# Cross attention and a 4-bit feed-forward layer on one core: block turns of the row and weight tiles by VectorE, their high parts stored by ScalarE

## The reference

```python
x = x + xattn(layernorm(x), ctx, ctx, mask, wq, wk, wv, wo)   # 32 query heads, 8 key heads of 128, rotary embedding, softmax
x = x + ffn(layernorm(x), qweight, lut4, lut8, bias)          # weights looked up from bit planes: 4 bits per weight
```

## Time and profile before

| | us |
|---|---|
| median of the runs before (3 runs) | 2351.77 |
| lowest and highest run | 2350.05, 2352.4 |
| span of the profiled execution | 2348.6 |
| median above that span | 3.17 |
| TensorE busy | 2330.7 (99%) |
| VectorE busy | 1690.5 (72%) |
| ScalarE busy | 1115.5 (47%) |
| GpSimd busy | 570.1 (24%) |

### The profile page before, as it was taken

One profiled execution on the slowest core, in us unless ns is written; L12 is line 12 of the kernel. 1 busy time (PEld: TensorE's weight loads), 2 busy tenths in 40 slices (PEclk: granted clock), 3 DMA queues, 4 the chain that ended last, 5 costly groups with the idle time before them and its releaser, 6 DMA issues.

```text
span 2348.6 us, 35132 instructions
## 1 busy us (share of the span) xinstructions
PE 2330.7 (99%) x11878; PEld 1989.3 (85%) x11878; DVE 1690.5 (72%) x3808; ACT 1115.5 (47%) x2469; POOL 570.1 (24%) x674
## 2 busy tenths in 40 slices
PE   9999999999999999999999999999999999999999
PEld 8999998788888888888888888888888888888787
DVE  7888777677776767777776767676777777776773
ACT  5555544555464646455544445444544444443110
POOL 1000001222232223232322232223323232322220
PEclk9999999999999999999999999999999999999999
DMA  7466558533344343434457633333333333335442
GB/s 258 159 199 213 190 177 299 170 109 117 115 133 120 109 127 111 129 107 128 117 162 238 209 104 115 90 112 109 112 93 113 105 100 111 107 93 185 122 142 81
DMA packets 330098, 328.26 MB, mean 140 GB/s; under 512 B 32448, under 2 KB 266176, under 8 KB 329920
## 3 DMA queue, kind: packets, MB, share of 16 engines
q1 hardware_dynamic: 294496, 309.88, 42.8%
q10 hardware_dynamic: 35424, 16.14, 2.6%
HBM read 181.73 MB, written 71.30 MB: 108 GB/s over the span
## 4 chain that ended last, share of the span: by engine, by line
PE 92%; DVE 3%; DMA 3%; ACT 1%; SPq 1%; issue 1%; POOL 0%; ACTq 0%; DVEq 0%
PE bank L829 28%; PE bank L915 28%; PE bank L845 7%; PE bank L886 7%; PE bank L783 7%; PE bank L955 7%; PE bank L760 7%; DMA small_split<-probs 1%; DMA k_scratch<-small_split 1%; SPq L615 0%; POOL probs L1930 0%; DMA small_split<-k_scratch 0%; DVE residual L1804 0%; PE bank L721 0%; PE bank L741 0%
## 5 line engine op out<-in xcount | busy, mean ns | idle before, releaser
L915 PE MATMUL bank<-weights_split,small_split 128*128 128x512 f32 x3072 | 741.0, 390 | 1.9 <-DVE small_split L1788 1.9
L829 PE MATMUL bank<-acts_split,weights_split 128*128 128x512 f32 (+1 forms) x3168 | 742.9, 384 | 0.0
L915 PEld LDWEIGHTS bank<-weights_split,small_split 128*128 128x128 f32 x3072 | 574.4, 188 | 121.6 <-DVE small_split L1788 3.2
L829 PEld LDWEIGHTS bank<-acts_split,weights_split 128*128 128x128 f32 x3168 | 575.1, 188 | 110.6
L1930 POOL TENSOR_SCALAR probs<-probs,row_numbers 128x256 f32<-128x256 f32 x512 | 359.3, 714 | 1192.9 <-DVE row_numbers L1774 1192.9
L1248 ACT ACTIVATE probs<-bank,row_numbers 128x256 f32<-128x256 f32 x512 | 238.1, 472 | 125.2 <-DVE row_numbers L1769 125.0
L1778 DVE STREAM_TRANSPOSE probs<-probs 128x512 f32<-128x512 f32 x250 | 177.7, 711 | 145.2 <-POOL probs L1930 145.2
L1922 POOL TENSOR_TENSOR rope_x<-rope_x,sin_t 128x512 f32<-128x512 f32 (+1 forms) x132 | 166.7, 1263 | 404.7 <-ACT rope_x L1221 404.5
L1763 DVE CUSTOM_DVE_ANT_0 bank<-bank,mask_tile 128x256 f32<-128x256 f32 x512 | 207.2, 447 | 64.5 <-PE bank L845 64.4
L1783 DVE TENSOR_TENSOR small_split<-small_split 128x512 fp32r<-128x512 f32 x250 | 178.8, 715 | 85.2 <-ACT small_split L1261 85.0
L845 PEld LDWEIGHTS bank<-small_split 128*128 128x128 f32 x1536 | 217.6, 190 | 23.0 <-DVE small_split L1743 1.6
(11 more groups left out here) (124 smaller groups left out, 2167.0 us busy)
## 6 DMA issues: line engine op xcount, KB each, us to landing
small_split<-probs SPq DMA_DIRECT2D x754, 64.0 KB, 2.2
raw<-in_L_xattn_wq SPq DMA_DIRECT2D x61, 512.0 KB, 3.8
raw<-in_L_xattn_wo SPq DMA_DIRECT2D x60, 512.0 KB, 3.8
k_scratch<-small_split SPq DMA_DIRECT2D x64, 256.0 KB, 2.3
v_scratch<-small_split SPq DMA_DIRECT2D x32, 512.0 KB, 2.9
x_scratch<-raw SPq DMA_DIRECT2D x64, 256.0 KB, 2.8
acts_split<-x_scratch SPq DMA_DIRECT2D x32, 512.0 KB, 5.0
mask_tile<-in_mask_BxSxS_ff SPq DMA_DIRECT2D x64, 256.0 KB, 3.0
```

What stands on the lines that cost most here:

```text
L829: last = pe.matmul(query_bank(j)[:, 0:wide], wq_s[:, h, c, a, :], xT[:, c, m, b * S:b * S + wide], start=c == 0 and i == 0, stop=c == C - ...
L915: last = pe.matmul(out_ps[part][:, :], o_s[:, a, u % 2 * S + t * P:u % 2 * S + (t + 1) * P], wo_s[:, h, m, n * BANK:(n + 1) * BANK], start ...
```

## The change

Rows 0 to 7 and all eight weight tiles are no longer turned by TensorE. VectorE turns each in two instructions, straight from the tile into two PSUM banks, in blocks of 32 x 32, reading the columns in an order (`block_order`) by which the blocks need no transpose of their own; each 32-row part is then stored by one DMA that spreads 32 partitions over 128 lines of 1 KB. The copies in DRAM and in `W` and `X` are laid out accordingly, the query products of the first half and the final layer's products read them in runs of 32 columns. The high part is stored first, by four DMAs that ScalarE issues after both of its copies, the low part by four DMAs of SP; both parts use one staging area in turn. Row 8 and the rows of the attention stage stay as they were. In the final layer, the first row's products are ordered by half, and the second row is turned after 32 of them.

```diff
 # ScalarE
+            def send_blocks(image, at, src, done):
+                for a in range(PARTS):
+                    act.dma_start(image[:, at + a * S:at + (a + 1) * S], src[a * QUAD:(a + 1) * QUAD, :]).then_inc(done, 16)
+            def blocks_high(e):
+                act.wait_ge(x_tr, 2 * e + 2)
+                act.wait_ge(x_stored, rows_stored(e))
+                for j in range(2):
+                    act.activation(x_split[:, j, :], x_ps[j][:, :], ACT.Copy).then_inc(x_hi, 1)
+                act.wait_ge(x_hi, 2 * e + 2)
+                send_blocks(x_blocks, (e // REP * 2 + HI) * REP * D + e % REP * D, raw, x_stored)
+                def weights_high(tile):
+                    act.wait_ge(w4_tr, 2 * tile + 2)
...
+                    for j in range(2):
+                        act.activation(weight_stage(tile, HI)[:, j * BANK:(j + 1) * BANK], w4_ps[j][:, :],
+                                       ACT.Copy).then_inc(w4_hi, 1)
+                    act.wait_ge(w4_hi, 2 * tile + 2)
+                    send_blocks(w_scr, (tile // REP * 2 + HI) * REP * D + tile % REP * D,
+                                weight_stage(tile, HI).bitcast(F32), w4_stored)
...
                 if b - 1 in V_ROW:
-                    x_high(V_ROW[b - 1], 0, x_ps[0])
+                    blocks_high(V_ROW[b - 1])
                 rope_swap(b * HKV, k_ps[0], 1.0, 0, 2)
...
                     if not (first or last) and g == TURN_AT[b]:
-                        weights_high(b - 1, D0)
-                    if not (first or last) and g == SECOND_AT[b]:
-                        weights_high(b - 1, D1)
+                        weights_high(b - 1)
                     if g + 1 < HKV:
                         rope_swap(b * HKV + g + 1, k_ps[(g + 1) % 2], 1.0, (g + 1) % 2, 2)
...
                         act.wait_ge(v_stored, 16 * (v_turn(b, i) + 1))
+                        act.wait_ge(w4_stored, 16 * 2 * PARTS * b)
...
 # VectorE
+            def turn_weight_blocks(tile):
+                dve.wait_ge(w4_ready, tile + 1)
+                dve.wait_ge(w4_lo, 2 * tile)
+                for j in range(2):
+                    dve.transpose(w4_ps[j][:, :], block_order(picks[0], j)).then_inc(w4_tr, 1)
+            def weights_low(tile):
+                dve.wait_ge(w4_hi, 2 * tile + 2)
+                if tile < NB - 1:
+                    dve.wait_ge(w4_stored, 16 * PARTS * (2 * tile + 1))
...
+                    if g == TURN_AT[b] - 1:
+                        turn_weight_blocks(b - 1)
                     if g == SECOND_AT[b]:
-                        weights_low(b - 1, D1)
+                        weights_low(b - 1)
...
+                if b in K_ROW and K_ROW[b] < HT:
+                    turn_row_blocks_early(K_ROW[b])
                 values_low(V0)
...
+                if b in V_ROW:
+                    turn_row_blocks_early(V_ROW[b])
                 values_low(V3)
 # TensorE
-                    if not (first or last) and g == TURN_AT[b]:
-                        turn_weights(b - 1)
...
-                if b in V_ROW:
-                    turn_row(V_ROW[b])
...
-                        xT[:, c, m, b * S:b * S + wide],
+                            moving = xT_blocks[:, b // 2, m, c, b % 2 * C:b % 2 * C + wide // QUAD]
...
+                if f == 0:
+                    products = [(0, c, k) for c in range(C) for k in range(3)]
+                    products += [(1, c, k) for c in range(C) for k in (0, 2)] + [(1, c, 1) for c in range(C)]
...
+                    if f == 0 and (n, c, k) == (1, C // 2 - 1, 2) and PE_ROWS > 1:
+                        turn_rows(1)
```

More of the change, by code:

```diff
@@ L734, in turn_rows @@
                 last.then_inc(ln_tr, 1)
-            def turn_weights(tile):
-                pe.wait_ge(w4_ready, tile + 1)
-                pe.wait_ge(stage_lo, STAGED // 2 + tile * STAGED)
-                for c in range(C):
-                    done = pe.transpose(w4_ps[c // 4][:, (c % 4) * P:(c % 4 + 1) * P],
-                                        picks[0][:, c * P:(c + 1) * P], ident[:, :])
-                    if c % 4 == 3:
-                        done.then_inc(w4_tr, 1)
             def batch(b, first=False, last=False):
@@ L794, in batch @@
                 values(0)
-                if b in K_ROW:
+                if b in K_ROW and K_ROW[b] >= HT:
                     turn_row(K_ROW[b])
@@ L948, in _ @@
                     pe.wait_ge(wide_free, B_WIDE - A_WIDE + f * NN + n + 1)
-                columns = [(n, c) for n in range(NN) for c in range(C)] if f == NT - 1 else [
-                    (n, c) for c in range(C) for n in range(NN)]
-                for n, c in columns:
-                    if f == 0 and n == 0:
-                        pe.wait_ge(w4_in[c], 16)
-                    for i, (a, m) in enumerate(PASSES):
-                        last = pe.matmul(out_ps[f % 2 * NN + n][:, :],
-                                         xT[:, c, a, f % HT * P:(f % HT + 1) * P],
-                                         w4_s[:, c, m, n * BANK:(n + 1) * BANK],
-                                         start=c == 0 and i == 0, stop=c == C - 1 and i == 2)
-                    if c == C - 1:
+                if f == 0:
+                    products = [(0, c, k) for c in range(C) for k in range(3)]
+                    products += [(1, c, k) for c in range(C) for k in (0, 2)] + [(1, c, 1) for c in range(C)]
+                elif f == NT - 1:
+                    products = [(n, c, k) for n in range(NN) for c in range(C) for k in range(3)]
+                else:
+                    products = [(n, c, k) for c in range(C) for n in range(NN) for k in range(3)]
@@ new lines, in _ @@
+                ends = [max(at for at, product in enumerate(products) if product[0] == n) for n in range(NN)]
+                for at, (n, c, k) in enumerate(products):
+                    a, m = PASSES[k]
+                    if f == 0 and at == 0:
+                        for piece in range(C // 2):
+                            pe.wait_ge(w4_in[piece], 16)
+                    if f == 0 and n == 1 and c == 0 and k < 2:
+                        for piece in range(2):
+                            pe.wait_ge(w4_in[C // 2 + 2 * k + piece], 16)
+                    last = pe.matmul(out_ps[f % 2 * NN + n][:, :],
+                                     xT[:, c, a, f % HT * P:(f % HT + 1) * P], w4_s[:, n, m, c],
+                                     start=c == 0 and k == 0, stop=at == ends[n])
+                    if at == ends[n]:
@@ L1707, in batch @@
                 values_low(V1)
-                if b in K_ROW:
+                if b in K_ROW and K_ROW[b] < HT:
+                    blocks_low(K_ROW[b])
+                elif b in K_ROW:
                     x_low(K_ROW[b], 1, x_ps[1])
```

205 lines of the change are left out of this document (107 added, 98 removed).

## The result

The changed kernel takes 2421.26 us (median of 4 runs, 2420.54 to 2425.06), the kernel before 2351.23 beside it: a ratio of 1.0297, with a 95% interval of 1.0282 to 1.0311. It is slower, by 70 us where 20 were forecast, and outside the range.

The account below looks back on a forecast made before the run. TensorE, busy 99% of the span, was taken to bound the kernel. New waits of 34.1 us less 13.9 us of turns removed gave +20 us on a median of 2351.8: 2372 us, range 2354 to 2384.

Parts of the forecast that it names:

- the mechanism of the waits: Projection stage: VectorE's turns and ScalarE's copies and 2.5 us issue burst delay the swap and cosine product that TensorE's key groups need.
- the first rival: ScalarE's bursts: issuing does not hold ScalarE, so waits of groups 2 to 4 vanish; 2345 us, chance 0.14.
- the second: ScalarE's bursts: an issue takes only 0.36 us, a burst 1.45; 2363 us, chance 0.15.
- batch 1: Projection stage: value product V2 starts late, behind VectorE's low parts and a landing store; 5.4 us.
- batch 2: Projection stage: row centring, bit copy and burst in one group delay key group 6, and V0's low part is late; 4.8 us.
- batch 6: Projection stage, one weight tile: the burst makes key group 4 stall 2.1 us.
- final layer: Second row turned after 32 products instead of 24: 1.8 us more, the third row's wait 4 us instead of 2.3.
- Batch 3: Projection stage: waits at key groups as in batch 4 (6.3 us), with the context copy 1 us later; 7.0 us.
- The contiguous loads I cost at nothing: Contiguous loads and wider store lines: no cost, since no wait for such a load stands in the chain.
- the sign of a wrong forecast: Attention stage: no difference expected; time coming there would show the forecast wrong.
- The third rival: VectorE becomes the bound at 1.9 us a pair, +9, 2381 us; or runs of 32 slow 1,536 query products, 6 us; chance 0.13.
- the pair of turns: VectorE: two block turns of 512 columns take 1.25 us, 20 us in all, with 1.9 us as the far end.

Follow-up runs that it names:

- e11: Kernel before, with 1,152 query products reading runs of 64 columns and 720 final products runs of 128: 2352.7 us.
- e7: Changed kernel with VectorE's turns reading 512 columns in one run instead of every fourth column: 2412.2 us.
- e1: Changed kernel with the four issues of each high part moved from ScalarE to SP's queue: 2394.9 us.
- e3: Changed kernel with the turns given back to TensorE, ScalarE's bursts of issues kept: 2395.5 us.
- e5: Changed kernel with both the high parts issued by SP and the turns given back to TensorE: 2380.6 us.
- e12: Changed kernel with SP's issues, turns and reads in one run, second final-layer row turned after 24 products, and row turns ahead of decoding: 2359.6 us.
- e9: Changed kernel with extra unread matmuls filling 16 of TensorE's waits in the projection stage: 2417.2 us.
- e6: Kernel before, with 1,152 query products and 720 final products reading 16 runs of 32 columns instead of one of 512: 2368.3 us.
- e8: Changed kernel with twelve test turns on VectorE at the start and the second final-layer row turned after 24 products: 2424.8 us, one run.
- e4: Changed kernel with each high part stored by one DMA of ScalarE over 128 partitions instead of four over 32: 2455.0 us.
- after: The changed kernel itself, as profiled, against the kernel before: 2421.3 us.

## Why the prediction was wrong, step by step

**Right.** The sign, and the mechanism of the waits: ScalarE is held (swap 0.1 us behind the last issue), which rules out the first rival; an issue takes 0.63 us, which rules out the second; the bursts took 2.5 to 2.8 us (four of the 16 3.0 to 4.1), and in four places the waits came as worked out: batch 1 6.3 us (5.4 forecast), batch 2 6.9 (4.8), batch 6 2.5 (2.1), final layer 3.7 (about 4). In all 40.4 us of new waits in the projection stage against 32.3. Batch 3, 6.9 against 7.0, is luck: 2.9 of it stand in front of key group 0, where none was forecast, and 4.0 at the groups that were to have it all. Of what the Trainium skill says (DMA: Bandwidth & Descriptors, Issuing engines are not separate DMA queues), that the time of an issue is "usually small relative to the DMA itself", the trace shows 0.63 beside 3.3 us to landing, and 14.8 us of the whole for 64 issues on the engine that others wait for: the rows were the better guide.

**Wrong, first: a term that was left at nothing.** "The contiguous loads I cost at nothing" looked at the loads, and the reads of TensorE in runs of 32 had a place only in a rival, at 4 ns over 1,536 products. The runs show 10 ns over 2,304: about 23 us, nearly half of the 49 us that were missed, most of it in the attention stage, where time was to be the sign of a wrong forecast. The 4 ns came from L886, which reads runs of 64; e11 shows that query products in runs of 64 cost nothing more, so that row said little of runs of 32. The third rival named both this and the dearer pair of turns, as alternatives to the forecast; both came on top of it.

**Wrong, second: the pair of turns.** 1.25 us was taken and 1.9 called the far end; it was 2.1 to 2.2. Both nearest rows read their columns in one run; the strided read was named in the prediction and given no price. e7: 9.0 us.

**Wrong, third: the sum of waits taken place by place.** The forecast counted the stall of each group from an engine that starts each batch on time. But VectorE had little room (busy 39.5 of 44.7 us in batch 1), and the burst and the turns together cost 11.5 us more than each alone (e1, e3, e5). The late turn of a row, with the next load, V1's copy and the next row's statistics behind it, was never followed, and the wait for the landing of the high part was named for the weight tiles and not for the rows. Both stand in the chain behind the 7.7 us of waits at the heads of batches 3 to 5; moving the turn forward gave back 4.3 (e12).

**Wrong, fourth: the clock, which had no term.** Behind most waits of 2 to 6 us the granted clock was at its lower level for a while (not behind the 2.54 us of batch 6), and key and value products took 14.7 us more. Of these 4 are shown to be time of the whole (e9), as a lower bound; for most of the rest the other engines were as late anyway.

The projection stage's 44 us are about 26 more than forecast. Read from the trace, 8.1 of them are waits, 14.7 longer key and value products, and some 3 are not placed. By the runs, the turns' price (9.0), the earlier turn (4.3) and the clock (4.1) make 17, if they may be added; that the rest is lateness which the two loads pass on to each other is argued from e1, e3 and e5 and not taken apart further.

## What to carry to other kernels

Before work leaves the busiest engine, ask what its output's new layout costs each later reader, times the number of reads: here 10 ns in 2,304 products, 23 us, outweighed the 13.9 us of turns, and they stayed in every version that kept these reads (attention stage of 1798 us or more, 1782 before). By e11 a layout with runs of 64 would not have this price; none was tried on the changed kernel. Where a second engine is busy for nearly nine tenths of the time, two new loads can cost more together than the sum of each alone; add one at a time, and follow each moved step to its loads as well as to its readers. For an operation with an access pattern that no row of the trace has, the nearest rows give a low end and not the price.

## What the runs showed of the hardware

- A matmul of 512 moving columns in 16 runs of 32 took 10 ns longer than in one run; in 8 runs of 64, or 4 of 128, no longer (e6, e11). The runs lay 1, 2 and 4 KB apart.
- A block turn of 512 columns by VectorE took 711 ns, with every fourth column read 1098; into PSUM 727 and 1114 (e8).
- An issue on ScalarE's queue took 0.52 us for a DMA over 128 partitions and 0.63 for one over 32 (e4, after); but the first, with four as the slowest dimension in DRAM, landed after 12.9 us in the place looked at, the others after 3.3 (median).
- Filling TensorE's waits kept its granted clock at 1.00 where it had been 0.62, and gave back 10.4 us of its busy time and 4.1 us of the whole (e9).
